# Perceiver block on one core: the shared network of its last layer as eight items of 128 inner units by 512 tokens, in three one-pass products, and the experts' down weights in one buffer

## The reference

```python
logits = jnp.einsum('bsd,ed->bse', hidden_states, gate_w)          # 16 experts
scores = jax.nn.softmax(logits, axis=-1).transpose(0, 2, 1)
topk_w, topk_idx = jax.lax.top_k(scores, cap)                      # cap = 8 tokens per batch and expert
x_tok = jnp.take_along_axis(hidden_states[:, None, :, :], topk_idx[..., None], axis=2)
g = jnp.einsum('becd,efd->becf', x_tok, Wg)
u = jnp.einsum('becd,efd->becf', x_tok, Wu)
h = jax.nn.gelu(g, approximate=False) * u
eo = jnp.einsum('becf,edf->becd', h, Wd) * topk_w[..., None]       # scattered back and added
gs = jnp.einsum('bsd,fd->bsf', hidden_states, Ws_g)                # shared network, 1024 inner units
us = jnp.einsum('bsd,fd->bsf', hidden_states, Ws_u)
shared = jnp.einsum('bsf,df->bsd', jax.nn.gelu(gs, approximate=False) * us, Ws_d)
```

## Time and profile before

| | us |
|---|---|
| three timed executions | 710.53, 710.9, 712.37 |
| the profiled execution: its time | 712.38 |
| its span, from the first to the last instruction | 710.6 |
| start of the router's product | 406.30 |
| start of the gather of tokens | 422.70 |
| start of the gate product of expert 1 | 446.17 |
| end of the value product of the last expert | 693.1 |

### The profile page before, as it was taken

One profiled execution on the slowest core, in us unless ns is written; L12 is line 12 of the kernel. 1 busy time (PEld: TensorE's weight loads), 2 busy tenths in 40 slices (PEclk: granted clock), 3 DMA queues, 4 the chain that ended last, 5 costly groups with the idle time before them and its releaser, 6 DMA issues.

```text
span 710.6 us, 10423 instructions
## 1 busy us (share of the span) xinstructions
PE 671.1 (94%) x4272; PEld 428.4 (60%) x4272; DVE 286.3 (40%) x595; ACT 240.1 (34%) x468; POOL 42.7 (6%) x43
## 2 busy tenths in 40 slices
PE   6699999999999999799998889999999999999996
PEld 5477777787877776478976474444444444444532
DVE  4845636445364354775876752111111111111112
ACT  4455536455453443355782122111111111111110
POOL 1800000000000000381000100000000000000000
PEclk9999999999999999999999999999999999999999
DMA  8111010110610000303076803899999999999911
GB/s 312 57 60 60 2 61 6 55 60 1 250 48 2 0 2 2 103 1 130 0 296 281 372 0 119 302 403 377 408 355 404 374 384 369 376 387 378 378 64 61
DMA packets 14348, 129.69 MB, mean 183 GB/s; under 512 B 2720, under 2 KB 2848, under 8 KB 6240
## 3 DMA queue, kind: packets, MB, share of 16 engines
q1 hardware_dynamic: 12384, 127.09, 46.2%
q10 hardware_dynamic: 1920, 1.97, 0.9%
HBM read 126.03 MB, written 1.05 MB: 179 GB/s over the span
## 4 chain that ended last, share of the span: by engine, by line
PE 82%; DVE 10%; ACT 4%; issue 1%; DMA 1%; SPq 1%; ACTq 1%; DVEq 0%
PE ps L959 23%; PE ps L1206 15%; PE ps L1238 8%; PE ps L1213 7%; PE ps L1245 4%; PE ps L1127 4%; PE ps L1032 4%; PE ps L1005 2%; PE ps L1043 2%; PE ps L1227 2%; PE ps L1164 2%; PE ps L1071 2%; PE ps L1176 1%; DVE stats L642 1%; DMA x<-in_x 1%
## 5 line engine op out<-in xcount | busy, mean ns | idle before, releaser
L855 DVE TENSOR_TENSOR hid<-hid,ps 128x256 f32<-128x256 f32 (+1 forms) x32 | 17.6, 553 | 141.6 <-PE ps L1206 91.4
L585 ACT ACTIVATE hid<-ps 128x256 f32<-128x256 f32 (+1 forms) x32 | 15.7, 490 | 141.6 <-PE ps L1213 86.5
L1238 PE MATMUL ps<-w_d,hid_T 128*64 128x512 f32 x256 | 58.4, 598 | 1.4 <-ACT hid_T L600 1.4
L1206 PE MATMUL ps<-w_u,x_slot 128*64 128x512 f32 x256 | 58.4, 598 | 0.0
L1206 PE MATMUL ps<-w_g,x_slot 128*64 128x512 f32 x256 | 57.8, 593 | 0.0
L476 ACT ACTIVATE probs<-ps,neg_max 128x512 f32<-128x512 f32 x64 | 43.5, 687 | 36.3 <-DVE neg_max L723 36.3
L959 PE MATMUL ps<-wv_hi,ctx_hi 128*128 128x512 f32 x128 | 52.3, 408 | 2.9 <-POOL wv_lo L395 2.9
L959 PE MATMUL ps<-wv_lo,ctx_hi 128*128 128x512 f32 x128 | 50.7, 396 | 0.0
L959 PE MATMUL ps<-wv_hi,ctx_lo 128*128 128x512 f32 x128 | 50.5, 395 | 0.0
L702 DVE COPY probs_T<-ps 128x512 f32<-128x512 f32 x32 | 22.1, 692 | 68.7 <-PE ps L1032 68.7
L723 DVE TENSOR_REDUCE neg_max<-ps 128x1 f32<-128x512 f32 x64 | 39.8, 684 | 20.2 <-PE ps L1005 20.2
(11 more groups left out here) (192 smaller groups left out, 1154.3 us busy)
## 6 DMA issues: line engine op xcount, KB each, us to landing
w_u<-in_wu SPq DMA_DIRECT2D x16, 2048.0 KB, 15.9
w_d<-in_wd SPq DMA_DIRECT2D x16, 2048.0 KB, 14.6
w_g<-in_wg SPq DMA_DIRECT2D x16, 2048.0 KB, 10.5
ctx_raw<-in_ctx SPq DMA_DIRECT2D x7, 1024.0 KB, 4.7
w_qkv<-in_wqkv SPq DMA_DIRECT2D x1, 3072.0 KB, 13.6
ws_g<-in_wsg SPq DMA_DIRECT2D x1, 2048.0 KB, 7.7
ws_u<-in_wsu SPq DMA_DIRECT2D x1, 2048.0 KB, 7.7
ws_d<-in_wsd SPq DMA_DIRECT2D x1, 2048.0 KB, 21.1
```

Source lines behind the costliest of these rows:

```text
L1206: ins = pe.matmul(ps[64 * fh:64 * (fh + 1), dst, :], x_slot[:, dt, e, :], weights[e % 2][:, dt, BANK * fh:BANK * (fh + 1)], start=(dt == 0 ...
L1238: ins = pe.matmul(ps[64 * fh:64 * (fh + 1), 6 + n % 2, :], hid_T[:, n % 2, j, 64 * fh:64 * (fh + 1)], w_d[e % 2][:, KT * fh + j, :], start ...
```

## The change

1. The shared network becomes eight items of 128 inner units for all 512 tokens. Gate and value have the weights' 128 columns as the standing operand and the tokens as the moving one, so the result is already transposed, and the transposes of shared items go. All three products are made of high and low parts: 12 one-pass matmuls of 512 columns each. The down product of an item writes four banks' worth in two pairs of banks; the third and the fourth part wait until DVE has added the first and the second one to x.
2. The parts are made on the way: ACT rounds a slice of the weights (`shared_high_gu`, `shared_high_d`), DVE takes the difference (`shared_low_gu`, `shared_low_d`), one item ahead, and the same for the hidden values (`hid_hi`, `hid_lo`) and for the layer's input (`xn_high(2)`, `xn_low(2, xn_lo_moe)` in the place of `ln_copy`).
3. The router's product is made of high and low parts too: 48 one-pass matmuls of 32 columns in the place of 16 float32 ones of 96.
4. ITEMS has 24 items: one shared item first, then one behind each odd expert from 1 to 13. Behind the gather the order of PE's work changes a little (the gate product of the second item ahead of the spread of the weights, its value product behind it).
5. For lack of memory w_d has one buffer. SP's order is g(e), u(e), d(e-1), and the load d(e-1) waits until the down product of expert e-2 is through. The last expert's down weights go into w_g0.

```diff
+            def downs_upto(n):
+                return experts_upto(n) + NT * shared_before(n + 1)
+        def shared_down_bank(n, t):
+            return (4, 6)[t % 2] + n % 2
...
-        SHARED = [("s", t, q * QUARTER, QUARTER) for t in range(NT) for q in range(4)]
-        ITEMS, REST = SHARED[:2], SHARED[2:]
+        SHARED = [("s", i) for i in range(NF)]
+        ITEMS, REST = SHARED[:1], SHARED[1:]
         for e in range(E):
             ITEMS.append(("e", e))
-            for _ in range(2 if e == E - 3 else 1 if 0 < e < E - 3 else 0):
+            if e % 2 and REST:
                 ITEMS.append(REST.pop(0))
...
-            for kind in "gud":
-                expert_load(kind, 1)
-            for e in range(2, E, 2):
-                for kind, ahead in (("g", 0), ("u", 0), ("g", 1), ("d", 0), ("u", 1), ("d", 1)):
-                    expert_load(kind, e + ahead)
+            def down_load(e):
+                if e == E - 1:
+                    sp.wait_ge(g_ps, AT["e", e - 1] + 1)
+                else:
+                    sp.wait_ge(down_ps, downs_upto(AT["e", e - 1]))
+                sp.dma_start(down_weights(e)[:], wd_d[e]).then_inc(wd_last_in if e == E - 1 else wd_in, 16)
+            expert_load("g", 1)
+            expert_load("u", 1)
+            for e in range(2, E):
+                expert_load("g", e)
+                expert_load("u", e)
+                down_load(e - 1)
+            down_load(E - 1)
...
+            def shared_high_gu(i):
+                if i:
+                    act.wait_ge(g_ps, AT["s", i - 1] + 1)
+                    act.wait_ge(u_ps, AT["s", i - 1] + 1)
+                act.copy(ws_g_hi[:], ws_g[:, :, shared_col(i)]).then_inc(ws_hi_done, 1)
+                act.copy(ws_u_hi[:], ws_u[:, :, shared_col(i)]).then_inc(ws_hi_done, 1)
+            act.wait_ge(gate_in, 16)
+            act.copy(gate_hi[:], gate[:]).then_inc(gate_hi_done, 1)
+            act.wait_ge(att_done, 2 * NT)
+            act.wait_ge(wsg_in, 16)
+            act.wait_ge(wsu_in, 16)
+            act.wait_ge(wsd_in, 16)
+            shared_high_gu(0)
+            shared_high_d(0)
             ln_std(2)
-            ln_copy(2)
+            xn_high(2)
...
             for n in range(2, LAST):
                 item_gelu(n)
+                after = ITEMS[n - 2]
+                split_next = after[0] == "s" and after[1] + 1 < NF
+                if split_next:
+                    shared_high_gu(after[1] + 1)
                 item_out(n - 1)
+                if split_next:
+                    shared_high_d(after[1] + 1)
...
+                    i = ITEMS[n][1]
+                    hi, lo = shared_parts
+                    pe.wait_ge(ws_split, 3 * i + off + 1)
+                    for dt in steps:
+                        w_hi_part, w_lo_part = hi[:, dt, :], lo[:, dt, P * i:P * (i + 1)]
+                        for j, (a, c) in enumerate(((w_hi_part, xn_hi), (w_hi_part, xn_lo_moe), (w_lo_part, xn_hi))):
+                            ins = pe.matmul(bank(dst), a, c[:, dt, :], start=(dt == 0 and j == 0),
+                                            stop=(dt == KT - 1 and j == 2))
...
+                    for t in range(NT):
+                        if t >= 2:
+                            pe.wait_ge(sx_done, NT * shared_before(n) + t - 1)
+                        rows = slice(P * t, P * (t + 1))
+                        for j, (a, c) in enumerate(((hid_hi, ws_d_hi[:]), (hid_lo, ws_d_hi[:]), (hid_hi, ws_d_lo[:, i, :]))):
+                            ins = pe.matmul(bank(shared_down_bank(n, t)), a[:, n % 2, rows], c, start=(j == 0), stop=(j == 2))
+                        ins.then_inc(down_ps, 1)
```

More of the change, by code:

```diff
@@ L33 @@
 KVW = 48
-LGW = 96
+LGW = 32
 EPS = 1e-5
@@ L931, in _ @@
             for n in range(2, LAST):
+                if not is_expert(n - 1):
+                    hidden_low(n - 1)
+                after = ITEMS[n - 2]
+                split_next = after[0] == "s" and after[1] + 1 < NF
+                if split_next:
+                    shared_low_gu(after[1] + 1)
                 item_hidden(n)
                 item_sum(n - 1)
+                if split_next:
+                    shared_low_d(after[1] + 1)
             item_sum(LAST - 1)
```

197 lines of the change are left out of this document (119 added, 78 removed).

## The result

The changed kernel takes **724.8 us** (median of four runs, 723.8 to 728.1) against 711.6 us of the kernel before beside it; the ratio is 1.019 with a 95% interval of 1.0156 to 1.0224. The forecast was 720.8 us, in a range from 707.0 to 730.0, and "slower": the sign and the range held, the size was 4 us short. The profiled execution of the changed kernel is the slowest of the four, 728.1 us; its mean granted clock was 0.969, that of the other three 0.973 to 0.979. Its span is 726.3 us against 710.6 before. These 15.7 us, 2.6 more than the medians differ by, lie in two places: the front (up to the gate product of expert 1, which starts 7.5 us later) and the experts' stage behind it (255.1 us instead of 246.9 from there to the end of the last value product, 8.2 us more).

A forecast was written before the change was run, and what follows sets the result against it. TensorE was taken to bound the experts' stage, with the loads only 8% behind. The terms -21.6 + 25.1 + 2.2 + 4.2 gave +9.9 us on 710.9, so 720.8 us, range 707 to 730.

The forecast's parts named there:

- Part 1: TensorE's own work in the experts' stage, with one-pass shared products: 21.6 us less.
- Part 2: Experts' stage: seven waits of 3.3 us ahead of odd experts' down products, 2.0 us at expert 14; +25.1 us.
- The eighth: Wait for down weights at expert 14, 1.0 to 2.2 us, taken as 2.0 us.
- the sentence that the bandwidth is no bound: Experts' stage: a pair's 12.6 MB need 30.8 us at 409 GB/s; the round of release, issue and landing binds.
- Part 3: Router and what stands around it: +2.2 us in all, the router's product ending 3.3 us later.
- low clock ends at about 410.6 us: Router's product: the half clock ends when it did before, after 2.5 us at half rate.
- Part 4: Splits into high and low parts are hidden under value and down products: nothing taken, first ones up to 0.5 us.
- Part 5: Experts' stage: the clock falls at two or three of the seven waits, +4.2 us (bounds 0 and 11.9).
- The short landing (707.1): Experts' stage: down loads land in 7.9 us, waits are 2.1 us each, clock keeps up, 707.1 us; chance 0.12.
- The rival with a clock fall at every wait (728.5): Experts' stage: clock falls at all seven waits, 11.9 instead of 4.2 us, 728.5 us; chance 0.14.

The follow-up runs named there:

- The run with thin shared items: Kernel before with three quarters of the shared network's products left out and all loads kept: 699.1 us, ratio 0.9807.
- the filled and the reordered front: Changed kernel with 12 unread wide products ahead of the router, 721.4 us; and with the first shared item's gate products moved there, 732.0 us.
- the filled kernel: Changed kernel with seven unread one-pass products added ahead of each odd expert's down product: 722.9 us, ratio 1.0141.

## Why the prediction was right in sign and short in size

**Part 1, TensorE's work.** Forecast −21.6, measured −15.9 in the sum above and −16.3 in the run without down loads, where a pair takes 31.28 us and the forecast had 30.6. The mechanism holds and the size was off: a one-pass product in the stage costs 0.234 us (and some 2.95 instead of 2.73 us for twelve with the hand-over), the shared down product 3.4 instead of 3.08 us.

**Part 2, the single buffer.** Forecast +25.1, measured +16.8. Seven of the eight places are right, the odd experts' down products, and the run with the single buffer alone shows that they need both parts of the change. The eighth, 2.0 us at expert 14, was not there: its load landed 9.5 us after its issue, and TensorE came later. The seven waits were 2.4 us each on the mean instead of 3.3, for two reasons. The landing was taken at 9.1 us; the changed kernel shows 7.7, 7.8, 9.3, 7.6, 10.0, 7.7 and 8.9, mean 8.4. The three long ones (9.3, 10.0, 8.9) are those where the load before was still 3 to 4 us from landing when they were issued (2.7 us or less for the other four), and the three long waits stand behind them. By the Trainium skill, DMA: Bandwidth & Descriptors (Anatomy of one DMA), whose fit is for another issuing path, it would be 6.8 us, an estimate; the shortest landing measured here, with nothing left ahead of it in the queue, is 7.6, 0.8 us more. And TensorE reached the odd down product some 0.3 us later than forecast, since its work in the gap was longer.

The step that failed in kind is the sentence that the bandwidth is no bound, with 30.8 us for a pair from 409 GB/s of one window. The run with thin shared items measures 33.2 us. The kernel before, at 33.55 us a pair, had 0.35 us of room in its steady stage, some 2.5 us over seven pairs. More could come only from loads that are ahead of TensorE when the stage begins, as in that run, whose stage was 14.2 us shorter. The changed kernel begins the stage with an empty queue instead (a window as above; DMA share 0.01):

```profile
455.80:465.00 9.20, 9.20 (x45) 3.02 (x42) 1.98 (x3) 2.11 (x4) 0.00 (x0) 1.00 0.01 2
```

A load of w_u landed at 455.8 us, and the next one, the down weights of expert 1, was issued only at 465.00, when expert 0's down product ended; the gate and value loads of expert 3 stood behind it in SP's list. This pause of 9 us was in no term of the forecast. Whether a second down buffer would have kept more of the gain is open: no run has the new shared items with two buffers.

The view that tells it was at hand, the window over one whole pair of the kernel before:

```profile
478.22:511.78 33.56, 33.56 (x150) 15.16 (x149) 4.98 (x8) 4.82 (x10) 0.00 (x0) 1.00 0.98 394
```

A DMA share of 0.98 over a whole period was as much as the queue with loads always waiting reached (97.9%); the rate of a good window is no measure of what the engines could do. The error did not show in the total: a pair of the changed kernel without a fall takes 33.1 us where I had 33.9. In that pair the odd expert's down load landed 5.1 us after the load before it (505.8 and 500.7 us), so the round of release and landing and the supply ended at nearly the same time.

**Part 3, the front.** Forecast +2.2, measured +7.5. Most of it is the router: forecast to end 3.3 us later (bounds 2.2 and 7.5), it ended 6.6 us later (418.15 against 411.55). The price at half clock was taken for a few us, since before it had come back after 3.4 us; it lasted 17. The failed step is "low clock ends at about 410.6 us": I carried a length over from products of another form. The router turned round took 5.9 us of the front back in its profile, and the filled and the reordered front show the clock falling under the small products without any wait.

**Part 4, splits hidden.** Right: no wait of TensorE for them; what is seen are waits of up to 0.2 us for x at five shared down products, 0.8 us in all.

**Part 5, clock in the stage.** Forecast 4.2 (2 or 3 falls of 1.7 each), measured 7.3 in the profiled execution: three falls, two of them twice as long. That waits are the cause is shown by the filled kernel, where there was none. The number of falls is partly luck: the waits were shorter than forecast and of two kinds, and the clock fell in the longer kind only.

**The rivals.** The short landing (707.1) asked for waits near 2 us and no loss elsewhere; the waits were short as it says, but front and clock took the gain back. The rival with a clock fall at every wait (728.5) had too many falls; what it said beside, 4 us more if the router's thin products don't bring the clock up, came near, the front being 5.3 us over. Of the measured 15.7 us against 9.9 the differences are: work +5.7, waits −8.3, clock +3.1, front +5.3, which give 5.8. The nearness of the total is partly luck: three errors of 3 to 6 us one way stood against one of 8 the other, and the medians, 13.1 us apart, are nearer to the forecast than the profiled executions.

## What to carry to other kernels

Before crediting an edit with the time that one engine saves, measure the next bound by itself: a run in which that engine's work is cut and all transfers stay costs one experiment and gives the floor at once; the DMA share over a whole period (0.98) hints at it even without. Look at the queue where the stage begins too: a wait in the issuing engine's list also holds back the loads behind it. A buffer may be given up where even the shortest gap between two uses covers a landing; count the gap in the new order, not in the old one. And small one-pass matrix products were dear twice here, for themselves and for the clock of what follows: it paid to turn the product so that the long side streams.

## What the runs showed of the chip that was not expected

- TensorE's clock was at half for 17.1 us on end with TensorE busy 15.5 us of them, over 48 products of 128x32 and what follows, and again with 128x96 columns; in four other profiles with the same router it was 17.1 us three times and 13.7 once. With wide products ahead it went up to full and fell again within the small ones, twice, without a gap between instructions.
- A small one-pass product of 32 columns follows the one before after 0.11 us at full and 0.21 us at half clock, so even small ones pay the clock nearly in full.
- A single load of 2 MB took 7.6 to 7.9 us when little or nothing was ahead; loads in a full queue landed every 5.54 us on the mean, and down loads in halves of 1 MB left the waits as long (17.3 against 16.8 us).
- Eight transfers of 16 KB each, issued from ScalarE, held its queue for 5.26 us, and the copy behind them with it.
